# The tokens' squared norms go through DRAM in another order, and the exponents are formed over contiguous rows

## What is computed

```
def _rfs(xw, ab, AB, gs):
    dot_products = jnp.einsum('...d,rd->...r', xw, ab[:, None] * gs)
    correction = (0.5 * jnp.sum(xw * xw, axis=-1))[..., None] * (ab * ab)
    return 1.0 / math.sqrt(NUM_RFS) * AB * jnp.exp(dot_products - correction)
...
xn = _layernorm(x, axis=-1)
s = einsum('bsr,or->bso', _rfs(xn, xis, exp(xis), proj_matrix), _rfs(input_weights, ...))
h = silu(tlin(xn, w1)) * tlin(xn, w2)
h = gelu(tlin(h, h1), exact)
h = gelu(tlin(h, h2), exact)
g = silu(tlin(h, w3))
out = x + s * g
```

## Time and profile before

| | |
|---|---|
| median of 3 runs | 1295.23 us (1295.19 to 1295.3) |
| the profiled execution's own time | 1296.77 us |
| its span, first to last instruction | 1295.0 us |
| mean granted TensorE clock | 0.999 of full speed |
| PE busy | 1284.7 us (99%) |
| DVE busy | 974.9 us (75%) |
| ACT busy | 762.0 us (59%) |
| POOL busy | 800.2 us (62%) |

### The profile page before, as it was taken

How to read it: one execution, slowest core, us unless ns; L and a number is a source line. 1 busy time by engine, 2 the same in 40 slices (tenths; PEclk the granted TensorE clock), 3 DMA queues, 4 the chain that set the end, 5 groups by cost and what they waited for, 6 DMA issues and landing times.

```text
span 1295.0 us, 16588 instructions
## 1 busy us (share of the span) xinstructions
PE 1284.7 (99%) x6066; PEld 1065.8 (82%) x6066; DVE 974.9 (75%) x1239; ACT 762.0 (59%) x1012; POOL 800.2 (62%) x804
## 2 busy tenths in 40 slices
PE   8999999999999999999999999999999999999997
PEld 7788888888888888888888888888888888888887
DVE  7888778778787777868777787777878777556675
ACT  4566655666556665565655656557565566555664
POOL 7964015999669995699947999388984890040000
PEclk9999999999999999999999999999999999999999
DMA  9698935455254541654416454265432644213441
GB/s 336 260 370 243 295 116 169 162 165 176 78 171 161 169 163 70 182 172 152 163 73 196 152 177 135 82 191 173 157 130 86 210 156 146 99 66 130 139 159 47
DMA packets 98199, 209.62 MB, mean 162 GB/s; under 512 B 14144, under 2 KB 17472, under 8 KB 97088
## 3 DMA queue, kind: packets, MB, share of 16 engines
q1 hardware_dynamic: 80176, 157.11, 36.2%
q0 software_dynamic: 17936, 51.39, 12.7%
HBM read 175.92 MB, written 38.83 MB: 166 GB/s over the span
## 4 chain that ended last, share of the span: by engine, by line
PE 98%; DVE 1%; ACT 0%; issue 0%; POOL 0%; POOLq 0%
PE ps L791 63%; PE ps L691 18%; PE ps L846 9%; PE ps L756 4%; PE ps L742 1%; PE ps L826 0%; PE ps L815 0%; PE ps L804 0%; PE ps L819 0%; PE ps L807 0%; PE ps L823 0%; PE ps L812 0%; PE ps L862 0%; DVE split L1330 0%; PE ps L680 0%; PE ps L880 0%
## 5 line engine op out<-in xcount | busy, mean ns | idle before, releaser
L791 PE MATMUL ps<-split,ring 128*128 128x512 f32 x3584 | 815.4, 389 | 0.0
L791 PEld LDWEIGHTS ps<-split,ring 128*128 128x128 f32 x3584 | 672.7, 188 | 139.7 <-DVE split L1324 0.4
L1324 DVE TENSOR_TENSOR split<-quad,split 128x1024 fp32r<-128x1024 f32 x224 | 290.4, 1305 | 143.3 <-ACT split L955 142.3
L955 ACT ACTIVATE split<-quad 128x1024 fp32r<-128x1024 f32 x224 | 231.5, 1052 | 42.1 <-PE ps L791 42.1
L691 PE MATMUL ps<-xT,w 128*128 128x512 f32 x1024 | 236.3, 391 | 1.0 <-ACT xT L1041 0.8
L691 PEld LDWEIGHTS ps<-xT,w 128*128 128x128 f32 x1024 | 190.9, 188 | 42.8 <-DVE quad L1318 2.0
L1000 ACT ACTIVATE quad<-quad,cols 128x512 f32<-128x512 f32 x192 | 136.5, 719 | 65.6 <-DVE quad L1355 38.0
L1347 DVE TENSOR_TENSOR quad<-quad 128x1024 f32<-128x1024 f32 x128 | 173.2, 1394 | 0.0
L537 POOL TENSOR_TENSOR ry<-ry,s 128x256 f32<-128x256 f32 x56 | 40.7, 759 | 200.7 <-issue 115.3
L938 ACT ACTIVATE rows<-ps,cols 128x512 f32<-128x512 f32 x128 | 87.2, 687 | 92.9 <-PE ps L691 47.2
L1318 DVE SCALAR_TENSOR_TENSOR quad<-ps,cols,rows 128x512 f32<-128x512 f32 x128 | 94.4, 745 | 47.4 <-ACT rows L938 30.7
(11 more groups left out here) (162 smaller groups left out, 1245.0 us busy)
## 6 DMA issues: line engine op xcount, KB each, us to landing
ring<-hs SPq DMA_DIRECT2D x428, 256.0 KB, 3.6
xin<-in_x SPq DMA_DIRECT2D x16, 512.0 KB, 4.2
s_h<-s SPq DMA_DIRECT2D x16, 512.0 KB, 4.5
seen<-in_h POOLq DMA_DIRECT2D x64, 128.0 KB, 2.9
ry<-in_x SPq DMA_DIRECT2D x15, 512.0 KB, 5.0
out<-ry SPq DMA_DIRECT2D x15, 512.0 KB, 2.6
z_h<-xin POOLq DMA_DIRECT2D x56, 128.0 KB, 3.8
xT<-z_h POOLq DMA_DIRECT2D x14, 512.0 KB, 6.5
```

The costliest lines, as they stand in the source:

```text
L791: mm = e.matmul(ps[:, 4 * (w % 2) + m, :], ring[n % RING][:, m * P:(m + 1) * P], slot[:, k, g, :], start=first and k == 0 and g == 0, stop ...
L955: e.activation(both(slots[i][:, :, 0, :], g), both(quad[at[t][L][name]], g), ACT.Identity).then_inc(hi, 1)
L1324: e.tensor_tensor(both(slots[i][:, :, 1, :], g), both(quad[at[t][L][FAST[w][1]]], g), both(slots[i][:, :, 0, :], g).bitcast(F32), ALU.subt ...
```

## The change

The DRAM buffer `q_h` is laid out block by block, `[NH, NB, P]` in place of `[NH, P, NB]`. The store of the columns becomes a transposing one: neighbouring numbers of a partition go to places 128 elements apart, so that its 512 numbers are 512 separate runs of one number each, where they were 128 runs of four. The load reads the same 512 numbers in one row, now in the order b * 128 + p. All 32 exponent instructions lose the rearranged views: their operands and output are plain rows of 512. The number of instructions, their order on each engine and their waits are the same.

```
-        q_h = nc.dram_tensor("q_h", [NH, P, NB], F32).ap()
+        q_h = nc.dram_tensor("q_h", [NH, NB, P], F32).ap()
...
-                e.dma_start(q_h[h], sm[:, 3, 4 * j:4 * j + 4]).then_inc(d_qout[j], 16)
+                e.dma_start(q_h[h].rearrange("b p -> p b"), sm[:, 3, 4 * j:4 * j + 4], allow_slow_non_contiguous=True).then_inc(d_qout[j], 16)
...
-                e.dma_start(qrow[j], q_h[h].rearrange("p b -> (p b)").partition_broadcast(P)).then_inc(d_qin[j], 16)
+                e.dma_start(qrow[j], q_h[h].rearrange("b p -> (b p)").partition_broadcast(P)).then_inc(d_qin[j], 16)
...
-                    e.scalar_tensor_tensor(out=q[r, j].rearrange("p (b q) -> p b q", b=NB), in0=qrow[j][:, :].rearrange("p (q b) -> p b q", b=NB),
-                                           scalar=ab2[:, r:r + 1], in1=src.rearrange("p (b q) -> p b q", b=NB),
+                    e.scalar_tensor_tensor(out=q[r, j], in0=qrow[j][:, :], scalar=ab2[:, r:r + 1], in1=src,
                                            op0=ALU.mult, op1=ALU.add).then_inc(seven_sum, 1)
...
-                        e.scalar_tensor_tensor(out=stage[n % 2][:, :].rearrange("p (b q) -> p b q", b=NB),
-                                               in0=qrow[j][:, :].rearrange("p (q b) -> p b q", b=NB), scalar=ab2[:, r:r + 1],
-                                               in1=ps[:, 4 + n, :].rearrange("p (b q) -> p b q", b=NB), op0=ALU.mult, op1=ALU.add).then_inc(dot_sum, 1)
+                        e.scalar_tensor_tensor(out=stage[n % 2][:, :], in0=qrow[j][:, :], scalar=ab2[:, r:r + 1],
+                                               in1=ps[:, 4 + n, :], op0=ALU.mult, op1=ALU.add).then_inc(dot_sum, 1)
```

## The result

| | median of 6 executions | lowest to highest |
|---|---|---|
| before | 1295.41 us | 1295.19 to 1296.47 |
| changed | 1302.55 us | 1300.42 to 1304.93 |

The ratio is 1.0054, with a 95% interval from 1.0042 to 1.0067: the change makes the kernel slower by 7.1 us. The forecast was 1295.2 us and no change.

The account below looks back on a forecast made before the run. PE was taken to bound the kernel, busy 1276.81 of 1278.00 us. Exponents, store and load each added 0, so the forecast was the median, 1295.2 us, no change, with a range of 1294.0 to 1296.5 for 8 in 10 runs.

Parts of the forecast that it names:

- What bounds the kernel: Whole kernel: PE holds 98% of the chain, busy 1276.81 of 1278.00 us, so other engines can give back at most 1.2 us.
- Part 1: The 32 exponent instructions on DVE: 745 ns each, 23.8 us in all, DVE down 13.2 us; 0 on the total time.
- Part 2: The store of the norms, 128 runs becoming 512: quiet landing up to 4.5 us, later landings hidden; 0 on the total time.
- The bound from above: Quiet landing of the norms' store in proportion to its runs: 4 x 3.1 = 12.4 us, still hidden.
- the 10 to 20 expected: Sign in tile 0: the norms' store, under loaded DMA engines, lands after 10 to 20 us.
- the 28 to 43 foretold: Sign in tile 0: norms_in(1), the load of the second half's norms, goes out between 28 and 43 us.
- 5.0 us ahead: Tiles 1 to 6: the feed issued at 381.84 lands in 3.6 us, 5.0 us before product w = 2 starts.
- The cover I named: Tiles 1 to 6: SP's wait for store_s and then the ring hides the late store; slips over 13.2 us would cost PE.
- The late row: Rival, tile 0: store scales with its runs under load, PE waits 21 us before the second mix; 1316 us, 11%.
- a joint slip of 17.5 us: Tile 0: the two norms' stores' joint lateness from which PE would wait before mix's second half; 14.6 us was forecast.
- The very late store: Rival, six tiles: quiet store landing after more than 16.3 us costs PE the excess; 1377 us at 30 us; 1% within 11%.
- The 19 times: Skill's factor for strided DMA transposes, applied to the 3.1 us landing: store takes 59 us, time an estimated 1550 us.

Follow-up runs that it names:

- sparse kernel: Against the changed kernel: each 4-byte run stored into its own 512-byte stretch, the exponents' row read from x; 1295.51 us, ratio 1.0001 to the kernel before.
- own4: Against the changed kernel: a partition's four 4-byte runs stored side by side, from a constant tile, row read from x; 1335.90 us, 1.0303 to the kernel before.
- group 5: Later runs on one chip: the changed kernel unaltered, 1320.08 us, ratio 1.0197 to the kernel before, beside two kernels with other places for the 4-byte runs.

## Why the prediction was wrong

**What bounds the kernel: right.** PE has no slack to give. The exponents alone changed 12 us of VectorE and no time.

**Part 1, the exponents: right.** 745 ns was forecast for all, 785, 747 and 748 ns were measured; the sum is 24.7 us against 23.8. The Trainium skill's statement (*Vector Engine (DVE) Microarchitecture Reference*, section 7) that the form with two SBUF sources that are not bf16 runs at half throughput is not borne out here: the 21 of that form take 785 ns, and those with one source in PSUM 747. VectorE's busy total did not fall to 962, though; it is 976.6, since other instructions took longer (the splitting subtraction L1324 took 290.4 us before, 301.6 after). With the exponents alone changed it fell to 964.8. Why L1324 took longer is open: in the sparse kernel, which loses nothing, it takes 299.4.

**Part 2, the store: this step failed, in two ways.** First, "at most 3.8 / 64 = 0.06 us a run, so 24 more runs cost up to 1.4 us: 4.5 us" priced the store by the number of its runs. It landed in 9.6. The count itself is as cheap as I said (sparse: 3.9 us), but the runs' places were never part of the sum. All rows I took prices from write runs of 128 bytes and more, and the stores of before 16 bytes; none puts a 4-byte run beside another. The bound from above, 12.4 in proportion, held the quiet landing, and the loaded ones (14.9 and 17.3 us, from 7.91 to 22.85 and 23.22 to 40.52) lay in the 10 to 20 expected.

Second, and this cost the forecast, I followed the late landing only to those who wait for it. That part of the working held: norms_in(1) went out at 40.52 in the 28 to 43 foretold, mix did not wait for the exponential, and the feeds of tiles 1 to 6 were not issued late. But the feed's landing was entered as 3.6 us, "5.0 us ahead". It took 9.64 in tile 3, 1.0 more than the 8.6 this leaves, and PE waited 0.9 us there; the feed of tile 0 took 9.95, and PE waited 1.5. And GpSimd's loads and stores in tile 0 did not appear in the sum at all, since nothing in them was changed; they account for the other 2.3 us of PE's waits. The cover I named, SP's wait, hides the store from SP. It hides nothing from the transfers that share the DMA engines with it.

**The rivals.** The late row gave the right sign by a mechanism that did not happen in the first measurement; its condition, a joint slip of 17.5 us, was not reached (40.52 + 7.0 = 47.5 for a row that was needed by 52.3). On the two later occasions it did happen, as a small part of the loss: norms_in(1) went out at 44.13 and 44.44, past the 43 foretold, and PE waited 0.5 and 0.4 us for ACT's exponential before the second half of the mix. The very late store did not happen in the changed kernel at first either; own4 shows it, with a landing of 16.74 us. The rule of the Trainium skill's *DMA: Bandwidth & Descriptors* (Rules for kernel authors) against a strided last dimension points at the loss, but its reason does not: one descriptor per element is what the sparse kernel has as well (its packets are as many), without a loss. The 19 times of the Trainium skill's *VectorE: DVE Perf Modes* (The three transpose paths) stands against the transposing hardware, which no run here uses. Taken against the plain store, as I took it, it is not what happened: the landing grew 2.5 times (3.9 to 9.6).

**What stays open.** The price differs: 7.1 us at first, 22.5 and 24.5 on two later occasions, 15.0 for the store alone on a third. Longer waits bring the lower clock with them and so widen the difference, but that the waits differ (4.7 us in the products at first, 12.9 in group 5) has a cause of its own. Whether that is the chip, or where the buffers lie in its memory, no run separates. What happens in the memory is argued from density and order, not shown: no record sees the writes themselves. Nor is the size of the stretch known in which neighbours disturb each other; for this store no loss is seen at 16 bytes, and a clear one at 8 only for a partition's own runs, which says how many runs fall together and not where a border lies.

## What to carry to other kernels

A small transfer is priced by more than its bytes, its runs and its landing: look at what shares the DMA engines while it is in flight, and in the trace at the bytes moved per slice. Don't store many 4-byte runs side by side into DRAM; turn them first where it is cheap (a transpose in blocks of 32x32 on VectorE, 212 ns for 128x32 numbers), so that one run is one piece, or give each run a place of its own if nobody has to read them in a row. A late transfer that makes the bounding engine wait can cost more than the wait, when the clock falls with it. And when PE holds 98% of the chain, 12 us of another engine are worth nothing, so the smallest risk outweighs them.

## What I had not expected of the hardware

- 512 writes of 4 bytes, 4 bytes apart, bring all DMA of the core down to 2 to 122 GB/s for about 5 us, beside a mean of 383 GB/s in the same window before. The same 512 writes 64 bytes apart land in 3.3 us, and the mean of that window is 385 GB/s.
- With the same density, it matters whose runs are neighbours: a partition's own four side by side cost 40.3 us in the whole kernel, runs of successive partitions side by side 24.5 us on the same chip. The one kernel with a partition's own runs side by side stores from another tile than the rest.
- After PE had waited 5.6 us, its granted clock was 0.50 until 80 us and full again by 82. A wait of 2.96 us halved it in the same kernel, one of 3.01 us in own4 left it at 1.00.
- The same kernel with such stores took 1302.55, 1318.04 and 1320.08 us on three occasions, while the kernel before stayed within 1295.4 to 1295.9 us by median on all.
